# A deformable-convolution kernel on one core: a deeper order of the steps on each engine, a wait inside GpSimd's gathers, and the sampling weights read from PSUM

## The reference

```python
# layer 0: group norm, deformable 1x1 convolution with bilinear samples, residual
offsets = conv2d(x, offset_w, offset_b, 1)           # 3x3, 8 outputs
mod = 1.0 + tanh(conv2d(x, mod_w, mod_b, 1))         # 3x3, 4 outputs
v = conv2d(x, kv_w, kv_b, 0)[:, C:]                  # 1x1
sampled = sample(v, grid + offsets) * mod            # bilinear, 4 corners
out = conv2d(sampled, out_w, out_b, 0)               # 1x1
x = x + out                                          # conv of gn(x)
# layer 1: group norm, ZCA whitening in groups of 16 channels over all images, residual
cov = einsum('gim,gjm->gij', xg, xg) / M + EPS * eye
x = x + einsum('gik,gk,gjk->gij', v, rsqrt(e), v) @ xg * weight + bias
```

## Time and profile before

| what | value |
|---|---|
| median of 3 runs | 8048.12 us (7969.8 to 8099.9) |
| the profiled execution, its time | 8024.76 us |
| its span | 8023.0 us |
| PE, DVE, POOL, ACT busy | 55%, 57%, 50%, 12% |
| mean granted TensorE clock | 0.766 |
| DMA | 1612 MB, mean 201 GB/s |

### The profile page before, as it was taken

How to read it: one execution, slowest core, us unless ns; L and a number is a source line. 1 busy time by engine, 2 the same in 40 slices (tenths; PEclk the granted TensorE clock), 3 DMA queues, 4 the chain that set the end, 5 groups by cost and what they waited for, 6 DMA issues and landing times.

```text
span 8023.0 us, 68116 instructions
## 1 busy us (share of the span) xinstructions
PE 4419.2 (55%) x16380; PEld 2691.4 (34%) x16380; DVE 4547.2 (57%) x10677; ACT 989.2 (12%) x2075; POOL 3998.9 (50%) x4115
## 2 busy tenths in 40 slices
PE   5555555455555555555555455455555533335876
PEld 3333333333333333333333333333333322223322
DVE  7666655566566556665665455455555534445654
ACT  1111111111111111111111111111111100000000
POOL 0366655565566556665665545544565555662000
PEclk9777777777777777777777777777777776667999
DMA  8766656566566566665665555555555533334999
GB/s 290 248 201 199 197 185 194 179 206 194 178 208 205 174 190 200 197 199 182 206 199 183 167 177 180 166 167 176 168 183 174 174 123 123 124 124 152 413 421 413
DMA packets 931572, 1612.45 MB, mean 201 GB/s; under 512 B 80944, under 2 KB 605872, under 8 KB 929456
## 3 DMA queue, kind: packets, MB, share of 16 engines
q0 software_dynamic: 196608, 537.13, 20.9%
q1 hardware_dynamic: 138928, 537.74, 20.4%
q10 hardware_dynamic: 595968, 536.90, 19.6%
HBM read 1074.58 MB, written 536.87 MB: 201 GB/s over the span
## 4 chain that ended last, share of the span: by engine, by line
another core or an unknown queue 41%; PE 18%; DVE 15%; issue 13%; ACTq 6%; ACT 3%; DMA 1%; DVEq 1%; SPq 0%
PE psO L989 10%; ACTq L1235 5%; DVE patch L583 5%; PE psA L957 4%; DVE patch L588 2%; DVE vring L474 2%; ACT sampT L1140 1%; DVE bst L407 1%; PE psG L1017 1%; ACT x1T L1158 1%; DVE taps L486 1%; DVE xr_mem L603 1%; PE psT L1003 1%; ACT vring L1123 1%
## 5 line engine op out<-in xcount | busy, mean ns | idle before, releaser
L856 POOL DMA_INDIRECT patch<-v,index_now x4096 | 3993.0, 975 | 3282.1 <-issue 1650.6
L989 PE MATMUL psO<-sampT,wO_sb 128*128 128x512 f32 x2048 | 1362.3, 827 | 1861.0 <-ACT sampT L1140 1469.4
L603 DVE SCALAR_TENSOR_TENSOR xr_mem<-psO,bo_sb,xr_mem 128x512 f32<-128x512 f32 x512 | 377.6, 749 | 2062.7 <-remote 1148.0
L957 PE MATMUL psA<-wB,xa_mem 128*128 128x364 f32 x3824 | 1375.3, 501 | 166.7 <-issue 77.1
L989 PEld LDWEIGHTS psO<-sampT,wO_sb 128*128 128x128 f32 x2048 | 530.8, 273 | 2542.4 <-issue 1825.1
L583 DVE TENSOR_TENSOR patch<-patch,weight 128x512 f32<-128x512 f32 x2048 | 1289.5, 692 | 5.6 <-DMA patch<-v,index_now 5.6
L957 PEld LDWEIGHTS psA<-wB,xa_mem 128*128 128x128 f32 x3824 | 749.7, 204 | 653.1 <-issue 262.5
L1003 PE MATMUL psT<-ident,xr_mem 128*128 128x128 f32 x2048 | 322.3, 309 | 1039.6 <-DVE xr_mem L603 780.1
L474 DVE TENSOR_TENSOR vring<-psA,biasB 128x256 f32<-128x256 f32 x956 | 401.1, 420 | 761.6 <-remote 528.6
L588 DVE TENSOR_TENSOR patch<-patch 128x512 f32<-128x512 f32 x1024 | 662.5, 688 | 28.6 <-issue 8.1
L1003 PEld LDWEIGHTS psT<-ident,xr_mem 128*128 128x128 f32 x2048 | 274.8, 161 | 1156.2 <-DVE xr_mem L603 766.3
(11 more groups left out here) (209 smaller groups left out, 2597.0 us busy)
## 6 DMA issues: line engine op xcount, KB each, us to landing
v<-vring ACTq DMA_DIRECT2D x128, 2048.0 KB
xa_mem<-x_dram SPq DMA_DIRECT2D x128, 1024.0 KB
xr_mem<-x_dram SPq DMA_DIRECT2D x128, 1024.0 KB
x<-xr_mem ACTq DMA_DIRECT2D x128, 1024.0 KB
xs_mem<-x_dram SPq DMA_DIRECT2D x112, 1024.0 KB
patch<-v,index_now POOLq DMA_INDIRECT x4096
patch<-x SPq DMA_DIRECT2D x64, 1024.0 KB, 13.5
out_dram<-patch ACTq DMA_DIRECT2D x64, 1024.0 KB, 32.8
```

The source lines that it names most:

```text
L603: eng.scalar_tensor_tensor(xr[m][j][:, o, :], psO[o][:, :], bo_sb[:, o:o + 1], xr[m][j][:, o, :], ALU.add, ALU.add)\
L856: eng.indirect_dma_start(out=patch[n][:, t, :], out_offset=None, in_=v2_flat[k], in_offset=bass.IndirectOffsetOnAxis(ap=index_now[n][:, t: ...
L957: mm = eng.matmul(conv_bank[wide][r][:, 0:NA], xa[m][j][:, c, r * W:(r + 1) * W], wB[:, c, :], start=(c == 0), stop=(c == CC - 1))
L989: mm = eng.matmul(psO[o][:, :], wO_sb[:, h, o * P:(o + 1) * P], sampT[:, h, :], start=(h == 0), stop=(h == CC - 1))
```

## The change

Three things are done.

1. **Deep order.** The steps of one sampled block are spread over more steps of the loop. With n the block that VectorE samples: TensorE does rows 0 and 1, `turn_x1` (n - 3), `out_conv` (n - 2), rows 2 and 3, `turn_samples` (n - 1), `gram_block` (n - 3). ScalarE copies the samples out (`samples_out`, n - 1) as the last thing of its step, and `x1_out` works on n - 3. VectorE samples the first half before `conv_out` of rows 0 and 1, adds the residual of n - 2 and the gram of n - 4. The order runs on over the ends of images (`image` has a fourth argument p, the image before), and is drained once, after the last.
2. **A wait in the batch.** After 8 of the 16 gathers of block n GpSimd waits for `psG_full` of block n - 6.
3. **Weights in PSUM.** `weights_in` copies the 256 weights of a pair from `weight` into 128 x 128 floats at the end of bank `psI`, once a pair for both blocks, and the multiplies read them there. The offsets' result, which was in `psI`, now lies in the unused columns of the bank of convolution row 3, which `place` gives free with its 19th step.

```diff
@@ the order of the steps
+        def ago(k, p, g, i, m, q, j):
+            jk = (j - k) % 2
+            d = (k - j + jk) // 2
+            mk = (m + d) % 2
+            if g is None or d == 0:
+                return None if g is None else (g, i, m, q, jk)
...
@@ VectorE, place and sample
-                eng.wait_ge(psI_full, use)
+                eng.wait_ge(off_full, b * NQ + q + 1)
...
+            def weights_in(i):
+
+                eng.tensor_copy(weight_now, weight[:, bass.ds(i * (2 * NJ * 4), 2 * NJ * 4)])\
+                   .then_inc(w_now, 1)
...
-                    w4 = weight[:, bass.ds((((i * 2 + j) * 2 + h) * NH + t) * 4, SHORT * 4)]\
-                        .unsqueeze(2).to_broadcast([P, SHORT * 4, CG])
+                    at = ((j * 2 + h) * NH + t) * 4
+                    w4 = weight_now[:, at:at + SHORT * 4].unsqueeze(2).to_broadcast([P, SHORT * 4, CG])
@@ GpSimd, gather
                 for t in range(NJ):
+                    if t == NH:
+
+                        eng.wait_ge(psG_full[j], b * PAIRS + i + GRAM_FULL - 2)
+                        alone(eng)
                     eng.indirect_dma_start(
@@ TensorE, one step of an image
-                            twice_before(turn_x1, 1 - m)
+                            if three is not None:
+                                turn_x1(*three)
+                            if two is not None:
+                                out_conv(*two)
...
-                            before(turn_samples)
-                            twice_before(gram_block)
-                            before(out_conv)
+                            if one is not None:
+                                turn_samples(*one)
+                            if three is not None:
+                                gram_block(*three)
@@ ScalarE, one step
+                        if one is not None and not (prepare and j == 0):
+                            samples_out(*one)
```

More of the change, by code:

```diff
@@ new lines, in run @@
+            image(None, 0, 1, 2)
+            with eng.Fori(1, B - 2) as b:
+                image(b - 1, b, b + 1, b + 2)
+            image(B - 3, B - 2, B - 1, None)
+            image(B - 2, B - 1, None, None)
+        def pairs(eng, pair):
+            for i in range(2):
+                pair(i, i, 0)
+            with eng.Fori(1, PAIRS // 2 - 1) as h:
+                for m in range(2):
+                    pair(eng.snap(h * 2 + m), m, h)
+            for i in range(PAIRS - 2, PAIRS):
+                pair(i, i % 2, i // 2)
@@ L232, in conv_of, with samples_turn, x1_turn @@
+        def samples_turn(b, i, j):
+            if isinstance(b, int) and isinstance(i, int) and b == i == j == 0:
+                return 0
+            return (b * PAIRS + i) * 4 + 2 * j - 1
+        def x1_turn(b, i, j):
+            end = isinstance(b, int) and isinstance(i, int) and (b, i, j) == (B - 1, PAIRS - 1, 1)
+            return (b * PAIRS + i) * 4 + 2 * j + (1 if end else 2)
         def conv_of(a, s, i, m, q):
             return (s, 0, 0, 0) if ends(i)[1] else (a, i + 1, 1 - m, q + m)
[L238 to L243, removed]
@@ L356, in pair @@
                         load_s(s, 0)
+                    if s is not None and not last:
+                        load_s(s, i + 1)
                     if g is not None:
                         load_r(g, i, m, q)
-                    if s is not None and not last:
-                        load_s(s, i + 1)
                 pairs(eng, pair)
@@ L485, in conv_out @@
                                           ALU.add)
-                    eng.tensor_tensor(taps[:, m, row + 1, :], bank[:, C:NA], biasB[:, C:NA], ALU.add)\
-                       .then_inc(psA_free[k], 1)
+                    ins = eng.tensor_tensor(taps[:, m, row + 1, :], bank[:, C:NA], biasB[:, C:NA],
+                                            ALU.add)
+                    if not (shared and row == QR - 1):
+                        ins.then_inc(psA_free[k], 1)
             def sum_taps(b, q, m, more):
@@ L634, in pair @@
                     for j in range(2):
+                        if g is not None:
+                            sample(g, i, m, q, j, 0)
                         if ca is not None and not (prepare and j == 0):
@@ L664, in image @@
                 pairs(eng, pair)
-                if g is not None:
+                if a is None and s is None:
+                    residual(g, PAIRS - 1, 1, PAIRS // 2 - 1, 0)
+                    gram_add(g, PAIRS - 2)
                     residual(g, PAIRS - 1, 1, PAIRS // 2 - 1, 1)
@@ L1033, in conv @@
                                 conv_rows(ca, ci, cm, cq, j, rows, g is None)
-                        def before(part):
-                            if j == 1:
-                                part(g, i, 0)
-                            elif not first:
-                                part(g, i - 1, 1)
-                        def twice_before(part, *ring):
-                            if not first:
-                                part(g, i - 1, *ring, j)
+                        one, two, three = (ago(k, p, g, i, m, q, j) for k in (1, 2, 3))
                         if g is None:
```

200 lines of the change are left out of this document (104 added, 96 removed).

## The result

The changed kernel takes 7319.12 us (median of 4 runs, 7303.95 to 7348.14); the kernel before took 8074.01 us beside it (4 runs, 7969.8 to 8319.24). The ratio is **0.914**, with a 95% interval of 0.905 to 0.924: 8.6% faster. I had forecast 7110 us, 11.7% under the kernel before, so the direction and the range held and the measured time is 209 us above the forecast. The profiled execution took 7348.14 us.

What follows compares the result with a forecast made beforehand. GpSimd was taken as the bound, its gathers, issue and index waits: 8024.8 less 1597.9 of index waits is 6426.9, plus 666 of new waits and 15 of draining makes 7108, say 7110 us; range 6400 to 7960.

Steps and rivals of the forecast that it cites:

- The frame: Whole kernel: the profiled 8024.8 us less 1597.9 of GpSimd's index waits, plus its new waits and 15 us of draining.
- R: GpSimd's waits in all 256 batches of the changed kernel, forecast at 666 us.
- the usual gap becomes one release: Between GpSimd's batches: fewer held signals leave a gap of 2.28 + 0.30 = 2.6 us; chance 0.40.
- the 5.8 us of part 1: Gap between GpSimd's batches in the deep order if signals are held as before: release, copies, row move and start.
- rival 2: Late signals unchanged and only moved: gaps of 5.8 us before every batch, 7927 us, down to 7600; chance 0.26.
- rival 1: Late signals all but end and GpSimd hardly waits between gathers: 6400 to 6500 us; chance 0.22.
- four signs of the forecast: In the trace: index waits 300 to 700 us, new gram waits, "remote" before sampT under 1000, gathers' mean 0.95 to 0.96.
- rival 3: VectorE samples before moving rows 0 and 1, gets them late, and the rest turns serial: 13.6 us gaps, 8925 us; chance 0.12.
- a swap of long gaps for short ones: GpSimd's wait inside the batch, where batches run together: a gap of 5 to 21 us becomes one of about 2.3.
- My 0.30 for each: Cost on GpSimd of each of the 256 added waits in the batch, bounded at 0 to 0.30 us.
- The holding: TensorE's signals are held back while GpSimd issues gathers, from about 8 us into a batch, and released when it pauses.
- not 61: VectorE's multiplies with weights in PSUM: they keep their length or lose up to 61 ns each, 125 us in all.

Runs made afterwards that it cites:

- e3: The changed kernel without the wait in the batch and with the weights read from SBUF, so the deep order alone: 7868.29 us, ratio 1.0015 to the kernel before.
- e1: The changed kernel without the wait inside the batch: 7945.72 us, ratio 1.014 to the kernel before.
- e5: The changed kernel itself, run again in another group: 7362.27 us, ratio 0.934 to the kernel before.
- e8: The changed kernel with GpSimd waiting, after 8 gathers, for their landing in place of the gram: 7278.36 us, ratio 0.923 to the kernel before.
- e6: The kernel before with only the wait inside the batch added: 7869.65 us, ratio 0.996.
- e12: The changed kernel with each gather fetching half of its elements, output not the reference's: 6248.17 us, ratio 0.989 to the kernel before.
- e7: The changed kernel with the sampling's adds reading their second operand from the weights in PSUM, output not the reference's: 7278.84 us, ratio 0.922 to the kernel before.
- e9: The changed kernel with GpSimd waiting after 4, 8 and 12 gathers for its own landings, not the gram: 8613.43 us, ratio 1.364 to the kernel before.
- e10: The changed kernel with the wait in the batch for the gram of block n - 4 in place of n - 6: 6489.91 us, ratio 1.028 to the kernel before.

## Why the prediction was right, and where it was off

**The frame held.** Time = 6426.9 + R + 15 gives 7429.9 with the measured R of 775.2 + 212.8 = 988.0 us, 82 above the profiled 7348.1; 48 of these are issue time (1602.3, not 1650.6), which I had held fixed, and 34 a single wait of GpSimd for samples, which the changed kernel doesn't have. So R was 322 us more than my 666, 82 came back elsewhere, and the median is 29 us under the profiled execution: that makes the 209 us.

**The step that was off** is the one in the forecast that says that "the usual gap becomes one release": R = 256 x 2.6 = 666. The measured R is 121 index waits of 6.4 us and 70 gram waits of 3.0 us, in 256 batches. The 3.0 us are near what I took; the 6.4 are more than the 5.8 us of part 1. In the gap of 6.74 us shown above the reason is that after the release ScalarE copies x1T first and TensorE's second transposes are yet to come. I had read the old gaps, where sampT was what ScalarE stood at, and priced the new ones with it as the thing released. By a count over the timeline, 134 of the 256 batches began after a gap of over 0.8 us, as in rival 2, 60 were stopped before the ninth gather, as in the forecast, 6 of them both, and 68 had neither, as in rival 1.

Of the four signs of the forecast two came as said: a new wait for the gram, and "remote" before sampT under 1000 us (644.2). The index waits, 775.2 us, are above my 300 to 700, and the gathers' mean did not fall.

**Part 1** was costed at nothing per batch, and alone it is nothing (e3, 1.0015). It moved the late signals from the residual (1148.0 to 411.2 us) to VectorE's rows (528.6 to 1198.7 us), which is the mechanism of rival 3. It did not get rival 3's price: the index waits are 6.4 us on the mean, and the longest is 15.7.

**Part 2** was called a swap of long gaps for short ones, and e1, e5 and e8 show that: 1583.1 us of index waits without the pause (on another chip), 770.3 with it and 251.0 of gram waits, 139.8 with one in every batch and 904.7 for the pauses. Two things I had not seen. Alone it does nothing (e6), because it must stand in an order in which the gram is late enough to be waited for. And a wait that is already met costs nothing: in e12, where none was waited for, an issue gap is (1534.8 - 286.8) / 4095 = 0.305 us, the same 0.30 as between all gathers. My 0.30 for each was too much.

**The holding** was read rightly for the kernel before, and is not the whole of it. Of the "remote" waits of ScalarE and VectorE over 3 us there, 270 of 361 ended while GpSimd stood still, 184 of them 2 to 3 us after its last gather, though it stands still for only a quarter of that time. In the changed kernel it is 162 of 328, in e8 117 of 292: the others ended while GpSimd was issuing. So a late signal often comes with a pause, but doesn't need one.

**Part 3** has two sizes. The gathers' mean did not fall to 0.95 to 0.96 us as I said it would. The 20 ns that the deep order adds hid the few that PSUM takes off, and the adds, which still read two SBUF inputs, keep the rest (e7, 949). The multiplies became 14 ns shorter each (692 to 678), not 61, which I had taken from another operation. The lateness of signals isn't from two SBUF inputs: e7 leaves no operation of the sampling with two SBUF inputs, and signals stay late. Why part 3 is nevertheless worth three points or more beside the pause, and costs 1.0% without it (e1 against e3), was not isolated beyond the 70 to 86 us of shorter gathers.

**What I missed altogether** is that the gain hangs on a condition outside of the kernel. The prediction took late signals as a property of the kernel. The kernel before took 7865 to 8074 us beside the change and e1 to e8, and 6308.7 beside e9 to e12, under my 6426.9 for R = 0; so R was most likely next to nothing there already (its trace there was not taken). That group ran on chip 0 and the others on 15 and 12; whether it is the chip or something else that goes on in it was not found: all I have is that e9 to e12 show no late signal, though GpSimd in e12 never pauses. So back-to-back gathers alone don't make signals late. Nor is the cause of late signals settled. Shown is that a pause of GpSimd shortens its waiting (e1, e5, e8), and that the two SBUF inputs of the sampling are not the cause (e7).

No version here is shown to beat both kernels under both conditions. e8 is the fastest that computes the reference where signals are late (0.989 of the change), and by the price measured in e9 some 12 to 16% slower than the kernel before where they are not.

## What to carry to other kernels

Where the trace shows an engine waiting for a signal whose sender is long done, look for what another engine does meanwhile, and try one pause in it: here the deep order and the pause, each worth nothing alone, gave 3.5% together, and 6.6 to 8.6% with the weights in PSUM. A wait makes a pause only if it is not already met, so look in the trace for its row before counting on it. And run the kernel before beside the new one each time: a gain that consists of slack against late signals is there only where signals are late.

## What the runs showed of the hardware

- TensorE's signals can reach the other engines over 10 us late while GpSimd issues indirect DMAs: the transposes that ended at 3008.18 were seen at 3020.63. Many come about 2 us after it pauses (2506.63 to 2508.75), many others while it issues (166 of the 328 long ones in the changed kernel).
- VectorE's signal to itself was late too: 193.7 us in 62 waits in e1, 45.9 in 22 in the changed kernel.
- This is not always so: the same kernel took 6308.7 us on chip 0 and 7865.48 to 8074.01 us in three other groups of runs, and no trace from chip 0 (e9 to e12) has a late signal.
- GpSimd goes on some 3 to 4 us after a gather if it waits for its landing: 3.32 us on the mean in e9, with signals on time, and 3.5 us in e8, where one wait took 5.69.
- GpSimd spends 0.95 us on an indirect DMA of 128 rows whether it fetches 128 or 256 numbers a row (median 944 ns in e12, 946 in e10).
